# Half-width mask products in a causal attention, with a second triangle table

## The reference

```python
attn = jnp.einsum('bhqd,bhkd->bhqk', q, k) / math.sqrt(HEAD_DIM)
attn = attn + alibi_bias(seq_len, N_HEADS)[None] + causal_mask(seq_len)[None, None]
attn = jax.nn.softmax(attn, axis=-1)
y = jnp.einsum('bhqk,bhkd->bhqd', attn, v)
...
scores = jnp.einsum('bqhd,bkhd->bhqk', xq, xk) / jnp.sqrt(jnp.float32(D))
scores = jnp.where(causal[None, None], -jnp.inf, scores)
attn = jax.nn.softmax(scores, axis=-1)
out = jnp.einsum('bhqk,bkhd->bqhd', attn, xv).reshape(b, s, e)
```

## Time and profile before

| | |
|---|---|
| timed runs, device us | 1726.06, 1743.94, 1743.99 |
| median | 1743.94 |
| span of the profiled execution | 1728.4 us (no own time beside the span is given for it) |
| mean granted TensorE clock | 0.941 |
| TensorE matmul busy | 1552.9 us (90%) |
| VectorE busy | 1245.4 us (72%) |
| ScalarE busy | 963.0 us (56%) |

### The profile page before, as it was taken

One profiled execution on the slowest core, in us unless ns is written; L12 is line 12 of the kernel. 1 busy time (PEld: TensorE's weight loads), 2 busy tenths in 40 slices (PEclk: granted clock), 3 DMA queues, 4 the chain that ended last, 5 costly groups with the idle time before them and its releaser, 6 DMA issues. The chain is left out here.

```text
span 1728.4 us, 32660 instructions
## 1 busy us (share of the span) xinstructions
PE 1552.9 (90%) x13324; PEld 967.6 (56%) x13324; DVE 1245.4 (72%) x1739; ACT 963.0 (56%) x1915; POOL 184.2 (11%) x263
## 2 busy tenths in 40 slices
PE   2798888989999999998899698899999999998997
PEld 0677654444434444877688586544444444356887
DVE  7676457888898861666488876688888988125897
ACT  5454334757768886545344322466686788744442
POOL 0233000000000000256001032000000000000000
PEclk9999958999999999999999898799999999779999
DMA  5000959100000000200100066840000000020000
GB/s 209 25 0 10 186 144 122 31 14 25 14 13 14 2 2 2 74 1 1 37 1 1 12 132 186 102 62 20 14 19 16 12 2 2 2 74 1 1 25 25
DMA packets 37877, 70.61 MB, mean 41 GB/s; under 512 B 5426, under 2 KB 13234, under 8 KB 36660
## 3 DMA queue, kind: packets, MB, share of 16 engines
q1 hardware_dynamic: 37732, 68.58, 17.7%
HBM read 48.90 MB, written 22.15 MB: 41 GB/s over the span
## 5 line engine op out<-in xcount | busy, mean ns | idle before, releaser
L1206 DVE TENSOR_REDUCE l_att_maxima<-psum 128x2 f32<-128x1024 f32 (+3 forms) x640 | 664.9, 1063 | 137.6 <-PE psum L1104 129.8
L1298 ACT ACTIVATE l_att_probs<-psum 128x512 f32<-128x512 f32 (+3 forms) x1280 | 605.8, 531 | 250.4 <-PE psum L1132 227.9
L1149 PE MATMUL psum<-l_att_probs,l_att_v 128*17 128x256 f32 (+2 forms) x4608 | 362.0, 387 | 1.2 <-ACT l_att_o L1305 0.7
L1132 PE MATMUL psum<-l_att_qt,l_kt 51*128 51x512 f32 (+6 forms) x1280 | 330.9, 470 | 7.5 <-ACT l_att_probs L1298 7.5
L1104 PE MATMUL psum<-l_kt,l_att_qt 59*128 59x512 f32 (+7 forms) x1280 | 286.2, 424 | 4.5 <-DVE l_att_maxima L1206 2.8
L1132 PEld LDWEIGHTS psum<-l_att_qt,l_kt 59*128 59x128 f32 (+1 forms) x1280 | 142.1, 193 | 173.9 <-ACT l_att_probs L1298 161.9
L1149 PEld LDWEIGHTS psum<-l_att_probs,l_att_v 128*17 128x17 f32 x4608 | 79.4, 96 | 149.5 <-issue 100.2
L1104 PEld LDWEIGHTS psum<-l_kt,l_att_qt 59*128 59x128 f32 (+1 forms) x1280 | 140.0, 201 | 18.9 <-DVE l_att_maxima L1206 18.0
L358 PE MATMUL psum<-xh,w_ternary 128*128 128x512 f32 x256 | 103.3, 404 | 17.9 <-PEq L165 16.3
L358 PE MATMUL psum<-xh,wgu_h 128*128 128x512 f32 x256 | 105.0, 410 | 13.5 <-DVE xl L156 5.0
L1101 PE MATMUL psum<-tri 64*128 64x128 bf16 x1024 | 90.0, 239 | 23.3 <-DVE l_att_maxima L1206 17.1
(11 more groups left out here) (203 smaller groups left out, 2498.7 us busy)
## 6 DMA issues: line engine op xcount, KB each, us to landing
l_kt<-qk_scratch SPq DMA_DIRECT2D x48, 256.0 KB, 11.2
qk_scratch<-l_att_kv_parts SPq DMA_DIRECT2D x22, 512.0 KB, 8.3
l_att_qt<-qk_scratch SPq DMA_DIRECT2D x168, 64.0 KB
qk_scratch<-y SPq DMA_DIRECT2D x10, 512.0 KB, 12.6
set_raw<-in_w_gu SPq DMA_DIRECT2D x2, 1024.0 KB, 7.0
y<-in_w_gu SPq DMA_DIRECT2D x1, 2048.0 KB, 8.6
raw_down<-in_w_dn SPq DMA_DIRECT2D x2, 1024.0 KB, 10.9
y<-in_rope SPq DMA_DIRECT2D x8, 256.0 KB, 6.5
```

The source lines that it names most:

```text
L1132: e.matmul(g.ps[:, i % SB, off:BLK], g.kt[rows_of(x), hp, kt * P:(kt + 1) * P], qt[rows_of(x), hp, off:BLK], start=u >= TPB, stop=True, sk ...
L1149: ins = e.matmul(g.ps[h * VW:h * VW + HD + 1, OB, lo:hi], g.v[:, kt, STEPS[st][1] * HG + h, :], pr[:, un % PB, h, lo:hi], start=u == 0 and ...
L1206: e.tensor_reduce(mp[:, st % 2, 2 * p:2 * p + 2, t, c], g.ps[:, bank:bank + 2, 0:w], AX.X, ALU.max).then_inc(s.mx, 1)
L1298: e.activation(pr[:, un % PB, h, off:BLK], g.ps[:, i % SB, off:BLK], ACT.Exp, scale=HD ** -0.5).then_inc(s.ex, 1)
```

## The change

The product of a half of the unit matrix with a triangle's half has only 64 columns that come from that half. The mask products are turned so that the half of the unit matrix is always the streamed operand, cut to its 64 columns, and the triangle's half the weight. Each of the two masks then writes its own 64 columns of PSUM, where both wrote all 128 before. For the maxima the weight was the triangle already. For the scores the roles of the operands change, which needs the transposed triangle: a second table, `earlier`, beside `later`. The two stored halves of the unit matrix shrink to one table of 64 columns. The first mask of a bank still opens it (`start=True`), the second doesn't.

```diff
--- before.py
+++ after.py
@@ -1063,6 +1063,18 @@
             ring = 0
             read = 0
 
+            def unit(rows):
+
+                return g.tri[rows, 0:HALF]
+
+            def later(rows, c):
+
+                return g.tri[rows, HALF + c * P:HALF + (c + 1) * P]
+
+            def earlier(rows, c):
+
+                return g.tri[rows, HALF + (2 + c) * P:HALF + (3 + c) * P]
+
             def open_slot():
 
                 if free[ring % 2] is not None:
@@ -1098,8 +1110,8 @@
                 for x in range(2):
                     half = slice(x * HALF, (x + 1) * HALF)
                     for m in range(2 if c == qb else 0):
-                        e.matmul(g.ps[:, bank + x, w - P:w], g.tri[half, (2 + m) * P:(3 + m) * P],
-                                 g.tri[half, m * P:(m + 1) * P], start=m == 0, stop=False, skip_group_check=True)
+                        e.matmul(g.ps[:, bank + x, w - P + m * HALF:w - P + (m + 1) * HALF], later(half, m), unit(half),
+                                 start=m == 0, stop=False, skip_group_check=True)
                 for x in range(2):
                     e.matmul(g.ps[:, bank + x, 0:w], qt[rows_of(x), pair, t * P:(t + 1) * P],
                              g.kt[rows_of(x), pair, c * BLK:c * BLK + w], start=c < qb, stop=True,
@@ -1127,8 +1139,8 @@
                     elif i < 2:
                         e.wait_ge(s.mx, mbase[1])
                     for c in range(2 if u < TPB else 0):
-                        e.matmul(g.ps[:, i % SB, off:off + P], g.tri[rows, c * P:(c + 1) * P],
-                                 g.tri[rows, (2 + c) * P:(3 + c) * P], start=c == 0, stop=False, skip_group_check=True)
+                        e.matmul(g.ps[:, i % SB, off + c * HALF:off + (c + 1) * HALF], earlier(rows, c), unit(rows),
+                                 start=c == 0, stop=False, skip_group_check=True)
                     e.matmul(g.ps[:, i % SB, off:BLK], g.kt[rows_of(x), hp, kt * P:(kt + 1) * P],
                              qt[rows_of(x), hp, off:BLK], start=u >= TPB, stop=True,
                              skip_group_check=u < TPB).then_inc(s.st, 1)
@@ -1517,7 +1529,7 @@
         g.x = sb("x_resident", [P, NT, D], F32)
         g.xh, g.xl, g.xn = sb("xh", [P, KD, BLK], F32R), sb("xl", [P, KD, BLK], F32R), sb("xn", [P, TPB, D], F32)
         g.cst = sb("consts", [P, 2 * P + BLK], F32)
-        g.tri = sb("tri", [P, 4 * P], BF16)
+        g.tri = sb("tri", [P, HALF + 4 * P], BF16)
         g.ident = g.cst[:, 0:P]
         g.identb = sb("identb", [P, P], BF16)
         g.mhalf, g.one_col, g.one_row = sb("mhalf", [P, TPB], F32), sb("one_col", [P, 1], F32), sb("one_row", [HALF // 2 + 1, P], F32R)
@@ -1588,8 +1600,10 @@
     mask[:, BLK - P:] = np.where(k > q, f32(NEG), f32(0))
     groups = (q // GROUP == k // GROUP).astype(f32)
     consts = np.concatenate([ident, mask, groups], axis=1)
-    later = np.where(q > k, f32(NEG), f32(0)).astype(f32)
-    tri = np.concatenate([np.concatenate([m[c * HALF:(c + 1) * HALF]] * 2, axis=0) for m in (ident, later) for c in range(2)], axis=1)
+    later, earlier = [np.where(m, f32(NEG), f32(0)).astype(f32) for m in (q > k, q < k)]
+    unit = np.concatenate([np.eye(HALF, dtype=f32)] * 2, axis=0)
+    tri = np.concatenate([unit] + [np.concatenate([m[c * HALF:(c + 1) * HALF]] * 2, axis=0)
+                                   for m in (later, earlier) for c in range(2)], axis=1)
 
     slope = (f32(4) * f32(2) ** (f32(-8) / np.arange(1, HEADS + 1, dtype=f32))).astype(f32)
     high = (slope.view(np.uint32) & np.uint32(0xFFFFF000)).view(f32)
```

## The result

The changed kernel took 1754.88 us (median of 4 runs, 1748.91 to 1761.41), the kernel before beside it 1736.63 (4 runs, 1726.06 to 1743.99): a ratio of 1.013, interval 1.0081 to 1.0179, so slower, by less than 2% (the two medians by themselves give 1.011). It lies above the predicted range of 1717 to 1749 us.

The account below looks back on a forecast made before the run. TensorE's own order was taken to set the pace in the attentions' regular steps. Gains of 4.85 us per attention, 9.7 in both, took the span from 1728.4 to 1718.7 us; plus 15.5 gave 1734.2 us, range 1717 to 1749.

Parts of the forecast that it names:

- What bounds the kernel: In both attentions, PE's own order sets the pace at full clock while maxima are made; other steps wait for VectorE or ScalarE.
- the price of a mask: Per group of four masks in the attentions, one shortened stream saved: 0.027 us at full clock, 0.055 at low clock.
- rival 1: Masks on one half stay 0.065 us apart at full clock, only the low clock's distance shrinks: 1742.4 us, chance 0.13.
- Rival 2: Both masks' streams count in each group: 19.4 us saved, 1724.5 us, a masked score place of 1.25 us; chance 0.08.
- the sum: Gains over an attention's 16 steps, 3.4, 0.15, 1.1 and 0.2 us: 4.85 us per attention, 9.7 in both.
- the term: First maxima and three steps of the first block: 56 groups at 0.04 us, halved for waits, 1.1 us per attention.
- the clock decides more than the masks: In an attention's last step, one fall to the lower clock costs 13.75 us, 41.3 us instead of 27.5.
- Rival 4: The clock falls in both attentions' last steps, costing 13.75 us more: 1748 us, slower than before; chance 0.16.
- The sentence on what would make the prediction fail altogether: It fails if the clock falls in places where it is full now, or the triangle's weight load exceeds 96 ns.
- The argument for an independent clock: Timed runs of the kernel before, 17.9 us apart, were read as a last-step fall that comes and goes between runs.
- The offset: Around the span: the timed median lay 15.5 us above the profiled span, carried over from 1718.7 to 1734.2 us.

Follow-up runs that it names:

- e1: Against the kernel before: score masks' operands turned as in the changed kernel, every mask still streaming 128 columns; ratio 1.0003, mean 1739.2 us.
- e8: The changed kernel again with 13 runs, against the kernel before: mean 1753.4 us against 1737.6, ratio of the means 1.009.
- e11: Against the kernel before: masks at 64 columns only in the first block of queries of each attention, 128 elsewhere; ratio 1.0047, mean 1740.9 us.
- e2: Against the kernel before: only the scores' masks at 64 columns, the maxima's at 128; ratio 0.9926, mean 1732.7 us.
- e5: Against the kernel before: masks at 64 columns only in each attention's nine regular steps, 128 elsewhere; four runs, ratio 0.9877, mean 1733.5 us.
- e7: Against the kernel before: all scores' masks at 64 columns, the maxima's at 64 only in the nine regular steps; ratio 0.9948, mean 1736.1 us.
- e10: e2 plus unread products in the attentions' last steps, against the kernel before: ratio 1.0017, mean 1729.9 us.
- e15: e5 plus unread products in the attentions' last steps, against the kernel before: ratio 0.9996, mean 1731.6 us.
- e9: e7 plus unread products in the attentions' last steps, against the kernel before: ratio 1.0004, mean 1737.8 us.
- e6: The kernel before plus unread products in the attentions' last steps, against the kernel before: ratio 1.0003, mean 1730.4 us.
- e3: Against the kernel before: only the maxima's masks at 64 columns, the scores' at 128 with turned operands; ratio 0.999, mean 1746.5 us.
- e4: The changed kernel plus unread products in the attentions' last steps, against the kernel before: ratio 1.0027, mean 1743.7 us.

## Why the prediction was wrong

- **What bounds the kernel, and the price of a mask.** Right. The distances came out as forecast (0.04 us between masks, 0.04 to the weight load, 1.28 us a place against 1.27, 0.33 us a regular step against some 0.4), and the turned operands and the table cost nothing (e1). The distance of 0.04 us contradicts rival 1. The rule behind it in the Trainium skill (TensorE: Matmul & The Clock Gate, section "Wait — 56ns, not 53.3ns?") is some 62 ns for each matmul, and it holds only with hardware decode off: with 0.04 us from mask to mask, the trace after shows that it doesn't bind here. The whole gain at equal clock was forecast as 9.7 us; it is 12.9 +- 1.5 in the first four runs and 11.0 +- 1.1 in e8. Rival 2's place of 1.25 us isn't there, and its 19.4 us are over both means, though the three e8 runs at 16.9 come near. That the gain is a little over the sum fits e11, where the first block alone gives 5.6 us against the 2.2 of the sum. By the sum's own prices a shortened stream counts double at the lower clock, and the clock was lower there for longer than the term assumed; that this is the reason wasn't tested.
- **The step that failed** is "the clock decides more than the masks". It was named rightly and sized wrongly. I let one thing vary, the clock in the last step of an attention, and kept it elsewhere as the one profile had it, with the sum taken at that clock. The runs show that the clock elsewhere depends on the change: the first block of the second attention was at 0.57 to 0.61 in three executions with the full change, where the old masks had 0.73 to 0.81; what follows was at 0.91 or 0.92, with the old masks at 0.94 to 0.98; and e11 shows that the first block's share comes from its own shortened masks. From the mean clocks of the two profiled executions the loss can be sized now: 0.941 - 0.907 = 0.034 of clock at 11.8 us for 0.01 is 40 us, less 12 us of gain is 28, and the spans differ by 25.2.
- **Rival 4** had the right sign, and a falling clock as its mechanism, but the wrong place: the last step of the first attention lost only 2.6 us, and its price of 13.75 us kept the high end of the range at 1749. The sentence on what would make the prediction fail altogether, a fall where the clock was full, is what happened. It had no rival and no price, though the earlier trace rows showed 0.70 and 0.83 in the first block: the place where PE was nearest to losing the clock, and where masks are the largest part of what it streams.
- **The argument for an independent clock** was wrong in part. The two timed levels of the kernel before were read as one fall more or less in a last step. Its runs in fact spread over 40 us. Chance is large, but its mean moves with the kernel.
- **The offset.** I carried 15.5 us from span to median. Each run's time is its span plus 1.8 us (1755.41 and 1753.6). The profiled execution of the kernel before had a clock of 0.941, where the mean of 118 runs is 0.935; at 11.8 us for 0.01 that is 7 of the 15.5 us. The rest was the chance of three timed runs: with a fourth their median fell to 1736.63.

## What to carry to other kernels

Where TensorE's clock already dips in a stretch, the columns that look wasted may be what holds it up, so the gain from removing them has to be set against the clock's price in that kernel (here 11.8 us for 0.01 against 11 to 13 us for all the masks). Record the granted clock with every timed run and compare kernels at equal clock; otherwise an 11 us gain and a 27 us loss (0.023 of clock in e8) are one number. Cut TensorE's work where it is busiest and leave it, or add unread work, where other engines hold it up. That last advice is argued, not shown: no version here beat both kernels beyond doubt. Three had an interval under 1 (e2 at 0.9926, e5 at 0.9877, e7 at 0.9948), but the means of all their runs are only 0.996, 0.996 and 0.999 of the kernel before, and with the unread products added (e10, e15, e9) none is faster. The unread products alone gained by their mean (e6, 7.2 +- 2.7 us), with a ratio of 1.0003.

## What the runs showed of the hardware

- The same program on the same inputs was granted between 0.921 and 0.954 of the full clock on average (118 runs on two chips), and its time followed with 11.8 us for 0.01.
- The second attention, with 51 rows in the operands where the first has 59, lost more clock than the first (from 0.81 to 0.57 between 1060 and 1160, from 0.74 to 0.69 between 200 and 300). The rows were not varied by themselves, so why is open.
- Taking 64 columns from the maxima's masks cost 0.010 +- 0.003 of clock (e3), from both 0.023 +- 0.003 (e8). From the scores' alone it cost nothing in e2 (0.001 +- 0.004), but some 0.008 +- 0.003 in e10 beside e6. Whether the whole is more than its parts is open.
- Unread products of 256 columns kept the clock full in 14 last steps out of 14 that were profiled, where seven of ten in the second attention fell without them, and raised the mean clock by 0.006 in both kernels (e4, e6).
- Two masks on one half of the array started 0.04 us apart with 64 columns and 0.07 with 128, at full clock.
